# Router scores of two expert layers: gate matrix as the loaded weights, tokens moving through four column quarters, scores turned on VectorE

## The chip, the cores and the metric

One core of a Trainium2 chip runs the whole kernel as one program. The metric is the device time of one execution in microseconds (us), compared by the median of several runs. TensorE (PE in the profile) multiplies; VectorE (DVE) and ScalarE (ACT) do elementwise work and copies out of PSUM, the memory that TensorE writes; GpSimd (POOL) computes small things and issues gathers; SyncE (SP) issues the plain transfers. PEld is TensorE's loading of weights, which has its own records.

## What is computed

The reference is a chain of six residual layers on 1024 tokens of width 512: a small feed-forward layer with a memory lookup, an attention without softmax, the feed-forward layer again, a mixture of experts, a rotary attention with softmax, and the mixture of experts again. The change touches only the router of the two expert layers:

```python
def _L1_ffn_ref(x, gate_w, w1, w2, w3):        # x: layer-normed tokens, gate_w: 8 x 512
    xt = x.reshape(-1, h)
    logits = xt @ gate_w.T                     # 1024 x 8, in float32
    probs = softmax(logits)
    top_vals, top_idx = top_k(probs, 2)
    top_vals = top_vals / sum(top_vals)
    ...                                        # each token goes through its two experts
```

The kernel takes the two largest of the eight logits of each token (the softmax keeps their order) and derives the two weights from their difference.

## The kernel before

Tokens are cut into `NT` = 8 tiles of `P` = 128, and the width of 512 into `C` = 4 chunks of 128. For each layer k, `HS[k]` is a pair: the normed tokens (token on the partition) and their transpose `HS[k][1]` (channel on the partition, token along the row). Every engine runs a program of its own in a fixed order, written out by hand; engines meet only at semaphores.

The work around the router, tile by tile, is:

- VectorE, in `dve_front`: the residual sum of a tile (L800 before the first expert layer, L1802 before the second), its statistics (L481), aggregation (L492 or L484), and two or three tiles later the normalisation (L488), after GpSimd has given the reciprocal deviation (L568, L569). Two iterations after a tile's normalisation comes `dve_top` for it (L594 and L595: the 8 sorted scores and their indices). The last two tiles' `dve_top` come at the very end; before the first expert layer eight small constants (L503 to L510) stand ahead of them.
- TensorE, in `pe_front` (L602): four transposes of a normed tile into PSUM; ScalarE copies them into `HS[k][1]` (L610). Then `pe_logits` (L586): for each of the four chunks one matmul whose weights are the 128 x 128 token block and whose moving operand is 8 columns of `gateT`. The result is 128 tokens by 8 scores, in the layout that `dve_top` reads directly.
- The order on TensorE before the first expert layer, in `pe_ffn0`: logits of tile i-2, then transposes of tile i, for i = 2 to 7, then logits of tiles 6 and 7. Before the second, in `pe_attn1`: four wide matmuls of the attention's output projection (L1675) for tile i-1, logits of tile i-5, transposes of tile i-4.
- `top_bank` gives two PSUM banks in turn; logits of tile i wait until `dve_top` of tile i-2 is done (`s_top`).

A float32 matmul instruction leaves two loads and two matmul records in the trace.

Behind the last `dve_top` comes the routing, one chain: `dve_moe` on VectorE (from L1224 on) ranks all tokens, TensorE inverts the permutation (L1090 to L1101), GpSimd gathers the first rows (L1056), they are transposed (L1107), and the experts begin (L1123). All engines close the layer before with `end_stage` on `stage_end`; SyncE then waits for `s_lgt` and starts to load the last of the four expert streams (L956, L967). [...]

`gateT` is stored 32 columns wide (`SR` = 32): columns 0 to 7 hold the gate matrix, the rest is zero. `NSTR` is 4. `NB32`, a tile of 256 words per partition, is used only later, in `dve_moe`.

Of the kernel before, what the change touches and what calls it, by code (L numbers as in the profile page):

```python
# [14 lines left out]
P = 128  # L15
T, D = 1024, 512
NT = T // P
C = D // P
# [15 lines left out]
NE, FF, TOPK = 8, 800, 2  # L34
SR = 32
NSTR = P // SR
# [13 lines left out]
def macaron_program(nc, A, out, stages=6):  # L50

    ctx = ExitStack()
    with ctx:
        def sb(name, shape, dt=F32):
            return ctx.enter_context(nc.sbuf_tensor(name, shape, dt))
# [48 lines left out]
        gateT = sb("gateT", [P, C, SR])  # L104
# [22 lines left out]
        PS = ctx.enter_context(nc.psum_tensor("PS", [P, 8, PSUM_F], F32))  # L127
# [14 lines left out]
        def S(name):  # L142
            if name not in sems:
                sems[name] = sem(name)
            return sems[name]
# [44 lines left out]
        HS = [(H1, HT1), (H1, HT1), (H2, HT2), (H2, HT2), (H1, HT1), (H1, HT1)]  # L190
# [42 lines left out]
        at = 2 * D + 2 * C * P  # L233
# [7 lines left out]
        def rtake(shape, dt=F32, parts=P):  # L241
            n = int(np.prod(shape))
            words = n if dt in (F32, U32) else (n + 1) // 2
            ap = RT[0:parts, rt[0]:rt[0] + words]
            rt[0] += words
            assert rt[0] <= 1160
            if dt != F32:
                ap = ap.bitcast(dt)
            if len(shape) > 1:
                names = "abcdefg"[:len(shape)]  # L250
                ap = ap.rearrange(f"p ({' '.join(names)}) -> p {' '.join(names)}",
                                  **{k: v for k, v in zip(names, shape)})
            return ap
# [9 lines left out]
        NB32 = rtake([NE, T // SR])  # L263
# [41 lines left out]
        at = 7584 + 2 * (2 * C * FF + FC * D)  # L305
# [159 lines left out]
        def instance(k):  # L465

            return SL[:k].count(SL[k])
# [4 lines left out]
        def dve_front(eng, link, k, update):  # L472


            lag = BEHIND[k]
            for n in range(NT + lag):
                if n < NT:
                    update(n)
                if 0 <= n - 1 < NT:
                    eng.wait_ge(s_x, NT * k + n)  # L480
                    eng.bn_stats(STAT[:, n - 1, :], X[:, n - 1, :]).then_inc(s_stat, 1)  # L481
                if n == NT and k == 5:
                    eng.wait_ge(s_stat, NT * k + n)
                    eng.bn_aggr(MV[:, n - 1, :], STAT[:, n - 1, :]).then_inc(s_moments, 1)  # L484
                if 0 <= n - lag < NT:
                    i = n - lag
                    eng.wait_ge(s_rstd, NT * k + i + 1)
                    eng.tensor_scalar(HS[k][0][:, i, :], X[:, i, :], MV[:, i, 0:1], RS[:, i:i + 1],  # L488
                                      ALU.subtract, ALU.mult).then_inc(s_h, 1)
                if 0 <= n - 1 < NT and not (n == NT and k == 5):  # L490
                    eng.wait_ge(s_stat, NT * k + n)
                    eng.bn_aggr(MV[:, n - 1, :], STAT[:, n - 1, :]).then_inc(s_moments, 1)  # L492
                if SL[k] == "moe" and n >= lag + 2:
                    dve_top(eng, link, k, n - lag - 2)
            if SL[k] == "moe":
                if instance(k) == 0:
                    dve_route_constants(eng, link)
                for i in range(NT - 2, NT):
                    dve_top(eng, link, k, i)
# [71 lines left out]
        def top_bank(k, i):  # L571

            return ((7, 4), (6, 7))[instance(k)][i % 2]

        def pe_logits(eng, k, i):

            f = instance(k)
            if f == 0 and i == 0:
                eng.wait_ge(S("s_gate"), 16)
                eng.wait_ge(S("s_sgl"), SL[:k].count("ffn0"))  # L580
                eng.wait_ge(S("s_ewc"), 2 * SL[:k].count("ffn0"))
            eng.wait_ge(s_ht, NT * k + i + 1)
            if i >= 2:
                eng.wait_ge(S("s_top"), NT * f + i - 1)
            for c in range(C):
                mm = eng.matmul(PS[:, top_bank(k, i), 0:NE], HS[k][1][:, c, i * P:(i + 1) * P], gateT[:, c, 0:NE],  # L586
                                start=(c == 0), stop=(c == C - 1))
            mm.then_inc(S("s_lgt"), 1)

        def dve_top(eng, link, k, i):  # L590
            f = instance(k)
            eng.wait_ge(S("s_lgt"), NT * f + i + 1)
            scores = PS[:, top_bank(k, i), 0:NE]
            link(eng.max(V8[:, i, :], scores))  # L594
            eng.max_index(I8[:, i, :], V8[:, i, :], scores).then_inc(S("s_top"), 1)  # L595

# [30 lines left out]
        def pe_ffn0(eng, k, f):  # L627
# [64 lines left out]
            for i in range(2, NT):  # L692
                if SL[k + 1] == "moe":
                    pe_logits(eng, k + 1, i - 2)
                pe_front(eng, k + 1, i)
            if SL[k + 1] == "moe":
                for i in range(NT - 2, NT):
                    pe_logits(eng, k + 1, i)
# [896 lines left out]
        def pe_attn1(eng, k):  # L1595
# [66 lines left out]
            for i in range(NT + 1):  # L1662
                if i < NT:
                    if i >= 2:
                        eng.wait_ge(S("s_ott"), i - 1)
                    for c in range(C):
                        tr = eng.transpose(PS[:, i % 2, c * P:(c + 1) * P], OTM[:, i, c * P:(c + 1) * P], ident[:])
                    tr.then_inc(S("s_ottr"), 1)
                j = i - 1
                if 0 <= j < NT:  # L1670
                    eng.wait_ge(S("s_ott"), j + 1)
                    if j >= 2:
                        eng.wait_ge(s_x, NT * (k + 1) + j - 1)
                    for c in range(C):
                        mm = eng.matmul(PS[:, 4 + j % 2, :], OTT[:, c, j * P:(j + 1) * P], WO[:, c, :],  # L1675
                                        start=(c == 0), stop=(c == C - 1))
                    mm.then_inc(S("s_wop"), 1)
                if i >= 5:
                    pe_logits(eng, k + 1, i - 5)
                if i >= 4:  # L1680
                    pe_front(eng, k + 1, i - 4)
# [261 lines left out]
```

## Time and profile before

| | us |
|---|---|
| median of 3 runs | 1244.46 |
| lowest and highest | 1243.29, 1249.1 |
| the profiled execution, its own time | 1242.31 |
| its span, from first to last instruction | 1240.5 |
| TensorE busy | 1152.3 (93% of the span) |
| VectorE busy | 866.3 (70%) |
| ScalarE busy | 352.7 (28%) |

Busy shares are means over stages with different limits. To judge an edit in two short stretches (about 160 to 179 us and 870 to 896 us), one reads these stretches: the chain of waits through them, and the instructions in order of time on TensorE and VectorE. [...]

### The profile page before, as it was taken

How to read it: one execution, taken by the hardware profiler on the slowest of the kernel's cores; microseconds unless marked ns; L12 is line 12 of the kernel's file. 1: busy time of each engine (PE TensorE's matmuls, PEld its weight loads, DVE VectorE, ACT ScalarE, POOL GpSimd, SP SyncE). 2: the span in 40 equal slices, each digit the busy share in tenths (PEclk: the TensorE clock that was granted, in tenths of full speed). 3: DMA queues.
4: the chain of work that ended last, by engine and by line, in shares of the span. 5: the costliest groups of instructions: out<-in, count | busy, mean ns of one | idle time of the engine just before them, and what ended most of it. 6: DMA issues, size and time to landing. Idle time of an engine off the chain costs nothing.

```text
span 1240.5 us, 28148 instructions
## 1 busy us (share of the span) xinstructions
PE 1152.3 (93%) x9930; PEld 521.7 (42%) x9930; DVE 866.3 (70%) x2483; ACT 352.7 (28%) x746; POOL 147.9 (12%) x223
## 2 busy tenths in 40 slices
PE   6799987999999999899899999999979899999992
PEld 3478563443333333444344444444624333333330
DVE  5832675877777774578889999942458678777754
ACT  5444610001010101322176777784110010101010
POOL 2220011011010101344000000000110010101010
PEclk9899979999999999999999999999899999999996
DMA  9100433158723436418704333006741655616566
GB/s 359 59 2 1 158 137 130 37 184 287 259 98 96 167 124 211 180 62 180 170 3 87 53 53 53 2 2 251 301 177 36 246 176 189 216 36 215 168 204 251
DMA packets 63668, 174.33 MB, mean 141 GB/s; under 512 B 9885, under 2 KB 16627, under 8 KB 61351
## 3 DMA queue, kind: packets, MB, share of 16 engines
q1 hardware_dynamic: 55471, 150.60, 37.5%
q0 software_dynamic: 5760, 18.88, 4.3%
q10 hardware_dynamic: 2296, 3.05, 0.7%
q8 instruction: 79, 1.29, 0.4%
q14 instruction: 62, 0.51, 0.1%
HBM read 785.47 MB, written 22.03 MB: 651 GB/s over the span
## 4 chain that ended last, share of the span: by engine, by line
PE 80%; DVE 9%; DMA 4%; issue 2%; ACT 2%; SPq 1%; POOL 0%; POOLq 0%; ACTq 0%; DVEq 0%
PE PS L1123 30%; PE PS L1142 14%; PE PS L1648 6%; PE PS L1635 5%; PE PS L1613 5%; PE PS L837 3%; PE PS L822 2%; PE PS L1675 2%; PE PS L1563 2%; PE PS L602 2%; DVE PS L1771 2%; PE PS L1568 1%; PE PS L586 1%; PE PS L1638 1%; DMA HH<-in_w 1%
## 5 line engine op out<-in xcount | busy, mean ns | idle before, releaser
L1123 PE MATMUL PS<-arena 128*32 128x400 f32 x3456 | 397.4, 502 | 8.1 <-DMA HH<-in_w 4.2
L1123 PE MATMUL PS<-HH,arena 128*32 128x400 f32 x1152 | 396.7, 502 | 0.0
L1123 PEld LDWEIGHTS PS<-arena 128*32 128x32 f32 x3456 | 147.3, 111 | 246.9 <-issue 238.8
L1313 DVE STREAM_TRANSPOSE arena<-arena 32x192 f32<-32x192 f32 x576 | 211.4, 367 | 7.2
L1771 DVE CUSTOM_DVE_ANT_0 PS<-PS,U 128x128 f32<-128x128 f32 (+7 forms) x256 | 186.7, 786 | 15.4 <-PE PS L1613 15.0
L1142 PE MATMUL PS<-arena 128*32 128x512 f32 x1512 | 192.3, 592 | 4.0 <-DVE arena L1313 4.0
L1291 DVE STREAM_TRANSPOSE arena<-arena 32x128 f32<-32x128 f32 x544 | 164.7, 303 | 16.7 <-DMA arena<-h_scratch,RT 8.8
L1718 ACT ACTIVATE arena<-PS 128x512 f32<-128x512 f32 (+3 forms) x384 | 160.1, 512 | 54.9 <-PE PS L1638 48.2
L1196 ACT ACTIVATE arena<-PS 128x400 f32<-128x400 f32 x72 | 36.2, 504 | 422.3 <-PE PS L1123 422.2
L1297 DVE TENSOR_TENSOR arena<-arena,PS 128x400 f32<-128x400 f32 x72 | 40.9, 571 | 128.6 <-ACT arena L1196 128.5
L1123 PEld LDWEIGHTS PS<-HH,arena 128*32 128x32 f32 x1152 | 126.1, 111 | 0.0
L1142 PEld LDWEIGHTS PS<-arena 128*32 128x32 f32 x1512 | 57.6, 110 | 123.7 <-issue 117.6
L1635 PE MATMUL PS<-arena 99*128 99x512 bf16 (+3 forms) x384 | 106.8, 328 | 1.1 <-ACT arena L1718 1.0
L1613 PE MATMUL PS<-arena 96*128 96x512 bf16 (+3 forms) x384 | 97.0, 327 | 2.8 <-DVE arena L1771 1.0
L1142 PE MATMUL PS<-HH,arena 128*32 128x512 f32 x216 | 98.6, 592 | 0.0
L1056 POOL DMA_INDIRECT arena<-h_scratch,RT x36 | 34.9, 968 | 376.7 <-DVE arena L1291 327.5
L1648 PE MATMUL PS<-arena 128*32 128x512 f32 (+3 forms) x768 | 76.2, 494 | 0.2 <-ACT HH L1725 0.2
L1635 PEld LDWEIGHTS PS<-arena 99*128 99x128 bf16 x384 | 36.7, 97 | 58.2 <-ACT arena L1718 26.9
L1066 POOL DMA_INDIRECT y_scratch<-arena,RT x36 | 35.3, 980 | 210.1 <-ACT arena L1208 205.9
L568 POOL TENSOR_SCALAR VE<-MV 128x1 f32<-128x1 f32 (+1 forms) x44 | 12.2, 277 | 403.6 <-DVE MV L492 368.4
L1563 PE MATMUL PS<-HH,arena 128*128 128x512 f32 x128 | 57.3, 608 | 1.7 <-ACT HH L610 0.9
L1208 ACT COPY arena<-PS 128x512 f32<-128x512 f32 x36 | 20.3, 587 | 121.9 <-PE PS L1156 73.5
(258 smaller groups left out, 1253.2 us busy)
## 6 DMA issues: line engine op xcount, KB each, us to landing
arena<-in_w SPq DMA_DIRECT2D x456, 800.0 KB
arena<-in_w2a SPq DMA_DIRECT2D x266, 768.0 KB
HH<-in_w SPq DMA_DIRECT2D x152, 800.0 KB
HH<-in_w2a SPq DMA_DIRECT2D x38, 768.0 KB
arena<-split_scratch SPq DMA_DIRECT2D x96, 128.0 KB, 6.3
arena<-y_scratch SPq DMA_DIRECT2D x24, 256.0 KB, 5.3
split_scratch<-arena SPq DMA_DIRECT2D x8, 768.0 KB, 4.8
arena<-in_wqkv SPq DMA_DIRECT2D x3, 1024.0 KB, 6.3
```

The lines of the kernel that those rows point to most:

```text
L837: mm = eng.matmul(PS[:, bank, jj * P:(jj + 1) * P], AT0[:, m % 4, j * P - a:(j + 1) * P - a], h_in[:, i, h * P:(h + 1) * P], start=(i == 0 ...
L1123: mm = eng.matmul(PS[SR * j:SR * j + SR, 2 * hf + m, 0:FH], XBT[:, u, c, SR * j:SR * j + SR], W13[j][:, c // 2, m, c % 2, hf * FH:(hf + 1) ...
L1142: mm = eng.matmul(PS[SR * j:SR * j + SR, y_bank(p), :], ACT_T[:, u, c, SR * j:SR * j + SR], half_of(j, half)[:, c % (FC // 2), :], start=( ...
L1291: tr = eng.transpose(XBT[SR * b:SR * b + SR, u, :, SR * a:SR * a + SR], src[:, :, SR * b:SR * b + SR])
L1297: eng.tensor_tensor(half, half, PS[:, 2 * hf + 1, 0:FH], ALU.mult).then_inc(S("m_act"), 1)
L1313: tr = eng.transpose(ACT_T[SR * b:SR * b + SR, u, :, rows], src[:, :, SR * b:SR * b + SR])
L1563: mm = eng.matmul(PS[:, at + par, :], WQKV[:, x, c, first:first + P], HS[k][1][:, c, J * HT_:(J + 1) * HT_], start=(c == 0), stop=(c == C ...
L1613: mm = eng.matmul(PS[:, b + lo // HT_, 0:hi - lo], QT[0:KS, slot, h, i * P:(i + 1) * P], KT[0:KS, slot, h, lo:hi], start=True, stop=True)
L1635: mm = eng.matmul(bank[:, 0:hi - lo], KT[0:KS + 3, slot, h, i * P:(i + 1) * P], QT[0:KS + 3, slot, h, lo:hi], start=True, stop=not diag, s ...
L1648: mm = eng.matmul(PS[32 * h:32 * h + 32, 7, lo - J * HT_:HT_], VA[:, i, (GH * g + h) * VC:(GH * g + h) * VC + 32], PB[n % NPB][:, h, 0:hi ...
L1718: eng.activation(PB[(n // GH) % NPB][:, h, 0:hi - lo], PS[:, EXP_BANK[u], 0:hi - lo], ACT.Exp, scale=SCALE1).then_inc(S("s_p"), 1)
L1771: eng.tensor_tensor_reduce(scores, scores, MASKW[:, T - wide:T], 1.0, HOLE, ALU.add, ALU.max, MP[:, g % 2, h, i:i + 1]).then_inc(S("s_md"), 1)
```

## The change

In `pe_logits` the operands change places. The weights are now the chunk of the gate matrix, 128 x 32, and the moving operand is 32 tokens of the transposed tile. The tile's 128 tokens are split in four groups; group j uses output partitions 32j to 32j+31, and with them a quarter of the array's columns. So a chunk takes four matmul instructions and a tile sixteen, where it took four. The result in PSUM is turned: partition 32j+e holds the score of expert e, column t the token 32j+t. `dve_top` therefore begins with one more VectorE instruction, which transposes each 32 x 32 block from PSUM into a part of `NB32`; `max` and `max_index` read that.

```diff
@@ pe_logits
             for c in range(C):
-                mm = eng.matmul(PS[:, top_bank(k, i), 0:NE], HS[k][1][:, c, i * P:(i + 1) * P], gateT[:, c, 0:NE],
-                                start=(c == 0), stop=(c == C - 1))
+                for j in range(NSTR):
+                    at = i * P + SR * j
+                    mm = eng.matmul(PS[SR * j:SR * j + SR, top_bank(k, i), 0:SR], gateT[:, c, :], HS[k][1][:, c, at:at + SR],
+                                    start=(c == 0), stop=(c == C - 1), skip_group_check=True)
             mm.then_inc(S("s_lgt"), 1)
@@ dve_top
             eng.wait_ge(S("s_lgt"), NT * f + i + 1)
-            scores = PS[:, top_bank(k, i), 0:NE]
+            turned = NB32.rearrange("p e b -> p (e b)")[:, SR * i:SR * i + SR]
+            link(eng.transpose(turned, PS[:, top_bank(k, i), 0:SR]))
+            scores = turned[:, 0:NE]
             link(eng.max(V8[:, i, :], scores))
             eng.max_index(I8[:, i, :], V8[:, i, :], scores).then_inc(S("s_top"), 1)
```

`link` makes the next VectorE instruction wait until this one is complete. No instruction changes its place among the others. On TensorE before the first expert layer, transposes (first row and third) alternate with the logits of a tile. Before:

```order
L602 MATMUL PS<-ident,arena 128x128 x4
L586 MATMUL PS<-gateT,arena 128x8 x4
L602 MATMUL PS<-ident,arena 128x128 x4
L586 MATMUL PS<-gateT,arena 128x8 x8
L1090 MATMUL PS<-RT,trib 128x72
```

and now:

```order
L606 MATMUL PS<-ident,arena 128x128 x4
L588 MATMUL PS<-arena,gateT 32x32 x16
L606 MATMUL PS<-ident,arena 128x128 x4
L588 MATMUL PS<-arena,gateT 32x32 x32
L1094 MATMUL PS<-RT,trib 128x72
```

The 4 instructions of a tile became 16 at the same place, the 8 of the last two tiles 32. On VectorE, in the same stretch, an iteration of `dve_front` with its `dve_top` was:

```order
L488 TENSOR_SCALAR arena<-X,MV,RS 128x512
L492 BN_AGGR MV<-STAT 128x2
L594 MAX RT<-PS 128x8
L595 MAX_INDEX RT<-RT,PS 128x8
L800 SCALAR_TENSOR_TENSOR X<-PS,arena,X 128x512
```

and is now:

```order
L488 TENSOR_SCALAR arena<-X,MV,RS 128x512
L492 BN_AGGR MV<-STAT 128x2
L596 STREAM_TRANSPOSE RT<-PS 128x32
L598 MAX RT<-RT 128x8
L599 MAX_INDEX RT<-RT 128x8
L804 SCALAR_TENSOR_TENSOR X<-PS,arena,X 128x512
```

The transpose stands between the tile's aggregation and its `max`, 16 times in the program. ScalarE, GpSimd and SyncE keep their programs.

## Rows read from the trace of the kernel before

**Rows 1.** Chain that ended last, 150 to 215 us: start us, us, what.

```profile
162.71 0.65 DVE X L800
...
167.69 1.51 PE PS L586 x8
...
178.31 0.19 DVE RT L594
...
178.96 0.30 DVE RT L1224
```

**Rows 2.** The same chain, 840 to 930 us.

```profile
870.71 0.79 PE PS L586 x8
...
892.43 3.23 PE PS L586 x16
...
896.34 0.30 DVE RT L1224
```

**Rows 3.** Stretches: us, busy of PE, PEld, DVE, ACT, POOL; then granted clock.

```profile
155.00:166.00 11.00, 8.30 (x49) 5.51 (x47) 10.29 (x30) 2.35 (x4) 4.49 (x11) 1.00 0.25 95
166.00:179.00 13.00, 11.69 (x56) 11.59 (x56) 6.06 (x35) 2.35 (x4) 1.58 (x4) 0.50 0.22 81
197.00:200.00 3.00, 3.00 (x20) 0.85 (x16) 2.88 (x10) 0.61 (x1) 0.40 (x1) 0.50 0.29 87
```

**Rows 4.** VectorE and ScalarE in order of time: start us, us, what [idle before <-releaser].

```profile
162.26 0.17 DVE L594 MAX8 RT<-PS 128x8 f32<-128x8 f32 x1 [0.54 <-PE PS L586]
...
162.62 0.73 DVE L800 SCALAR_TENSOR_TENSOR X<-PS,arena,X 128x512 f32<-128x512 f32 x1
...
889.94 0.55 DVE L488 TENSOR_SCALAR HH<-X,MV,RS 128x512 f32<-128x512 f32 x1 [0.40 <-POOL RS L569]
...
175.09 0.59 ACT L610 COPY arena<-PS 128x512 f32<-128x512 f32 x1 [1.87 <-PE PS L602]
```

**Rows 5.** TensorE in order of time, 166 to 179 us, same columns.

```profile
169.05 1.09 PE L602 MATMUL PS<-ident,arena 128*128 128x128 f32 x4
169.94 1.72 PE L586 MATMUL PS<-gateT,arena 128*128 128x8 f32 x8
...
173.96 1.09 PE L602 MATMUL PS<-ident,arena 128*128 128x128 f32 x4
```

**Rows 6.** TensorE, 200 to 201 us: three of four quarters in two rounds.

```profile
200.43 0.51 PE L1123 MATMUL PS<-arena 128*32 128x400 f32 x3
...
200.77 0.51 PE L1123 MATMUL PS<-arena 128*32 128x400 f32 x3
```

**Rows 7.** TensorE, 273.9 to 274.7 us: first and last of 16 in a burst.

```profile
274.01 0.61 PE L1156 MATMUL PS<-arena,ACT_RING 32*32 32x512 f32 x1
...
274.12 0.61 PE L1156 MATMUL PS<-wu1T,ACT_RING 32*32 32x512 f32 x1
```

**Rows 8.** TensorE, 844 to 846.1 us: quarters (L1648) and whole array in turn.

```profile
843.67 1.04 PE L1648 MATMUL PS<-arena 128*32 128x512 f32 x8
844.64 0.28 PE L1635 MATMUL PS<-arena 99*128 99x256 bf16 x1
...
845.73 0.23 PE L1635 MATMUL PS<-arena 99*128 99x128 bf16 x1
845.80 0.22 PE L1638 MATMUL PS<-mask_st,identb 128*128 128x128 bf16 x1
845.95 1.50 PE L1648 MATMUL PS<-arena 128*32 128x384 f32 x24
```

**Rows 9.** VectorE by form: busy us, mean ns | idle before: its transposes.

```profile
L1291 DVE STREAM_TRANSPOSE arena<-arena 32x128 f32<-32x128 f32 x544 | 164.7, 303 | 16.7 <-DMA arena<-h_scratch,RT 8.8
L1310 DVE STREAM_TRANSPOSE ACT_RING<-arena 32x32 f32<-32x32 f32 x144 | 29.2, 203 | 2.7
```

**Rows 10.** TensorE, 187.4 to 188 us: small matmuls on the whole array.

```profile
187.44 0.57 PE L1101 MATMUL PS<-arena 128*128 128x54 bf16 x16 [2.73 <-DVE arena L1257]
187.86 0.38 PE L1085 MATMUL PS<-identb 128*128 128x512 bf16 x1
```

## The prediction

> **What bounds the kernel now.** TensorE is the busiest engine over the whole span, but an edit in two short stretches is judged there, so the first view is the chain of waits through the stretches in which the routers work.
>
> Before the first expert layer [rows 1] the chain runs on VectorE up to about 166.6 us (its rows are sums, statistics and normalisations like the first one shown). From there to 178.31 it is on TensorE without a break: transposes and router matmuls in turn, 1.51 us for a tile of logits. Before the second layer [rows 2] it is on TensorE earlier, where projections alternate with tiles of logits of 0.79 us; the last two tiles of logits take 3.23. Both times the routing (L1224, at 178.96 and 896.34) starts only when the last tile is ranked, and nothing of the experts can start before it.
>
> [...] In the slow stretch weight loading is busy 11.59 of 13 us: these matmuls cost the loading of 128 columns of tokens; their 8 moving columns are nothing beside it. The change goes at the right term.
>
> The third view is TensorE in order of time [rows 5]: a period is (173.96 - 169.05)/2 = 2.46 us, of which the transposes have 0.89 and a tile of logits 1.56, counted from start to start. By the same way of counting 0.79 at full clock is some 0.82.
>
> **What a tile of logits costs afterwards.** Sixteen instructions make 32 pairs, in 8 rounds of four quarters. The trace has no pair with 32 loaded and 32 moving columns, so I bound it. The experts' quarters take 0.34 us a round for 400 columns [rows 6], by columns 0.027 for 32. A load of 32 columns is a quarter of the 0.10 us (0.79/8) of one of 128, 0.025. Starts are 7 ns apart: 16 small pairs start from 274.01 to 274.12 [rows 7], 0.027 for four. All three agree if load, matmul and starts overlap; I take 0.03 a round and 0.24 for eight. The upper end are 16 whole-array matmuls of 54 and 36 columns, which take 0.42 us, 26 ns each whatever their columns [rows 10]: 32 x 0.026 = 0.83.
>
> Changing between whole array and quarters has a price too. L1638, with 128 bf16 columns (half of the 0.12 that 256 need), is followed by the first quarter of L1648 after 0.15: 0.09 more than its columns. The other way, L1635 starts 0.97 after the first of two rounds of 512 columns, each 0.34 x 512/400 = 0.43: 0.11 more [rows 8]. I take 0.19 a tile. A block is 0.19 + 0.24 = 0.43 against 0.82: **0.39 saved at full clock**. At half clock I double the rounds (0.45, without margin) and take 0.30 for the two changes, between 0.19 and 0.38: 0.75 against 1.55, **0.80 saved**.
>
> **What the transpose costs.** VectorE turns 32 x 32 elements in 203 ns and 32 x 128 in 303 [rows 9]. Here it is 32 elements per partition, on all partitions and out of PSUM; with `link` around it I take 0.24 us, the ends being 0.20 and 0.37. Maximum and index take 0.36 us (162.26 to 162.62, [rows 4]) as before, so a ranking is 0.60.
>
> **First expert layer.** In the VectorE part three transposes add 0.72. Against it, VectorE waits 0.54 us for the first logits [rows 4], and that block ends 0.39 earlier: net +0.33 by 167 us. Only +0.1 of it reaches tile 4's transposes on TensorE, since the third transpose lies behind that tile's normalisation. The next tile's normalisation comes late by another 0.1. Then three periods of 0.90 + 1.55 become 0.90 + 0.75: -2.4. The loop through VectorE (logits, ranking, normalisation, next transposes) comes close behind TensorE within the same period. From the last transposes (173.96) to the last ranking (178.31) were 4.35 us. Now ScalarE's copy is waited for: it ends at 175.68 [rows 4], 1.72 after those transposes start; the last logits follow with 0.7, and latencies make it 2.5. VectorE's constants and the ranking before the last end at the same time. That is -1.85, and the last transpose adds 0.24. Sum: 0.2 - 2.4 - 1.85 + 0.24 = **-3.8 us**.
>
> **Second expert layer.** TensorE is the bound for the logits of tiles 0 to 2, between projections: 3 x 0.39 = -1.15. Then VectorE's iterations lead, with one more transpose in them, and tile 7's normalisation, at 889.94 before [rows 4], comes about 0.87 earlier. From it to L1224 were 6.4 us, most of it TensorE at half clock. Now it is 0.6 for the normalisation, 1.78 for transposes and copy, 0.7 for the logits, and 0.65 (178.31 to 178.96 in [rows 1]) + 0.24 for the ranking: 3.97, or -2.43. Sum **-3.3 us**.
>
> **What follows.** The routing, the gather and SyncE's load of the last weight stream all start on the end of the last ranking, so they shift together. Total -7.1: the profiled execution would take 1242.31 - 7.1 = 1235.2. It is 2.15 below the median of the three runs, so the median becomes 1244.46 - 7.1 = **1237.3**.
>
> **Rivals.**
>
> A. *The pair has a floor.* If each pair costs the 26 ns of [rows 10] in quarters too, and twice that at half clock, a block is 0.83 + 0.19 = 1.02 against 0.82, and 1.66 + 0.30 = 1.96 against 1.55. Some 5 blocks count at full and 8 at half clock, and 1.7 us of transposes: 5 x 0.2 + 8 x 0.41 + 1.7 = +6.0, **1250.5, slower than before**. If the floor does not double, 8 x (1.13 - 1.55) = -3.4 and the total is -0.7, 1243.8. The same sum, 1.7 - 5 x 0.63 - 8 x 1.25 + (5 + 16) x 32p, turns from gain to loss at p = 0.017 us a pair. Against it: 7 ns in [rows 7], though that is a burst of 16, not 32. Chance 0.12.
>
> [...]
>
> B. *Load and matmul of one quarter do not overlap* when both are this short: a round takes twice as long, 13.5 ns a pair. The same sum gives -2.4, 1242.1. For it: no row shows the overlap with so few columns. Chance 0.14.
>
> C. *The clock.* TensorE does less here, so the clock may fall one stretch earlier (0.5 and 0.9 us), or the experts' first matmuls, at half clock from 197 to 200 [rows 3], may stay there for longer, 1.7 us each time. That leaves 2.5 to 5.5 of the gain: 1239 to 1242. Chance 0.16. Experts that start at full clock would give 1.5 to 3 more instead, down to 1234; that is in my range.
>
> D. *It moves nothing*, since the experts' first matmuls wait for something with a time of its own, the weights or the token rows in memory: 1244.5. Against it: the load of the last stream waits for the same event. Chance 0.06.
>
> **Numbers.** The forecast has 0.52. 0.5% is 6.2 us, about what a measurement of this kernel can tell from no change; the border is 1238.2, only 0.9 from the forecast. Most of the forecast's chance and a little of C's lie beyond it: faster 0.50. The rest of the forecast, B, C, D and half of A are within: 0.44. Slower 0.06. The range goes from 1233.5, experts at full clock, to 1244, which leaves out most of A and D.
>
> **What would show it.** L588 as 32 starts a tile about 7 ns apart, blocks of 0.43 us at clock 1.00 and 0.75 at 0.50; a VectorE transpose of 0.20 to 0.25 us; from the start of the first tile's ranking to L1224 13.3 us instead of 16.7; TensorE idle between L588 and L606 in waits for VectorE. Starts 26 ns apart would prove A, 13 ns B, a clock of 0.50 ahead of 166 us or far into the experts C.

## The result, and the profile after

| | before | after |
|---|---|---|
| median of 21 runs of each, us | 1245.96 | 1237.17 |
| lowest and highest, us | 1239.39, 1249.39 | 1231.4, 1247.8 |
| profiled execution, us (span) | 1242.31 (1240.5) | 1238.7 (1236.9) |
| TensorE's granted clock over the span, as a share of its full speed | 0.971 | 0.976 |

The ratio after to before is 0.9938, with a 95% interval of 0.9924 to 0.9952: 7.7 us faster, or 6.0 to 9.5 (the medians differ by 8.8). The forecast was 7.1. Both the size and the sign held; what lies under them held only in part, and the experiments are mostly about that. That the median of 1237.17 lies so close to the 1237.3 forecast is luck in part: the kernel before came out at 1245.96 here, 1.5 above the 1244.46 that the forecast started from. The profiled execution was forecast at 1235.2 and took 1238.7.

First the chain that ended last, after, 150 to 215 us (start us, us, what). It answers to [rows 1].

```profile
165.30 0.44 PE PS L588 x32
165.77 0.23 DVE RT L596
...
172.28 0.66 PE PS L606 x4
172.94 0.44 PE PS L588 x32
173.40 0.23 DVE RT L596
...
177.87 0.30 DVE RT L1228
```

TensorE no longer holds the chain without a break. L588 is the new router matmul, L596 the new transpose, L606 the transposes on TensorE (L602 before), L1228 the routing (L1224 before). From the first ranking (165.77) to the routing it is 12.1 us; before it was 16.7.

The two stretches can be cut at events that both kernels have: the first from the start of tile 0's transposes on TensorE to the routing, the second from the second layer's first projection to the routing. Here they are for the kernel before (us; busy PE, PEld, DVE, ACT, POOL; then granted clock, DMA share, GB/s):

```profile
157.70:178.96 21.26, 18.24 (x100) 16.66 (x100) 13.65 (x56) 4.69 (x8) 4.73 (x12) 0.70 0.26 99
851.08:896.34 45.26, 43.79 (x184) 27.87 (x184) 17.68 (x57) 8.35 (x15) 6.51 (x16) 0.93 0.89 356
```

The same view of the kernel after:

```profile
161.57:177.87 16.30, 10.08 (x292) 6.67 (x292) 15.06 (x65) 4.69 (x8) 4.83 (x12) 1.00 0.36 132
849.65:891.19 41.54, 38.30 (x376) 20.33 (x376) 19.23 (x64) 8.36 (x15) 6.51 (x16) 1.00 0.97 388
```

The first stretch is 4.96 us shorter, the second 3.72. Weight loading has gone from 16.66 to 6.67 us and from 27.87 to 20.33; VectorE does 1.4 to 1.55 us more. What the sum of the forecast did not have is the last column but two, the granted clock: 0.70 and 0.93 before, 1.00 and 1.00 in this execution after. [rows 3] showed 13 us at half clock around the end of the first stretch; here there is none ahead of either routing.

The stretches shrink by 8.7 us together, the profiled executions differ by 3.6 only. The rest lies where nothing was changed: the first stretch begins at 157.70 before and at 161.57 after, and over the fourteen profiled executions told of here its start lies anywhere from 157.70 to 164.54. All that lies outside the two stretches adds up to 1171.2 to 1180.4 us over the fourteen (1174.0 before, 1179.1 after). So the stretches are the finer ruler below, with two limits: each kernel has one profile, and the time from a routing to the experts, which is told of further down, is not in them.

TensorE in order of time, after (start us, us, engine line, matmul, out<-in, count [idle before <-releaser]):

```profile
165.23 0.46 PE L588 MATMUL PS<-arena,gateT 128*32 128x32 f32 x32
165.62 0.66 PE L606 MATMUL PS<-ident,arena 128*128 128x128 f32 x4
166.21 0.46 PE L588 MATMUL PS<-arena,gateT 128*32 128x32 f32 x32
168.21 0.66 PE L606 MATMUL PS<-ident,arena 128*128 128x128 f32 x4 [1.55 <-DVE arena L488]
```

A block of 32 pairs is 0.39 us from its start to the next transposes' start (165.23 to 165.62). Record by record, the four quarters of a round start 7 ns apart and the next round starts 32 ns after the last one did (52 ns after the first round of a block). The last line has the wait that the prediction asked for: TensorE idle until VectorE's normalisation. Summed up by who is waited for, 161 to 178 us (waiting <- released by: us, times, longest):

```profile
PE PS L606 <- DVE arena L488: 5.2, 6, 1.5
```

and before, 157 to 179 us:

```profile
DVE RT L594 <- PE PS L586: 6.9, 6, 1.6
```

The wait has turned round. Before, VectorE stood 6.9 us waiting for logits and TensorE 3.3 us waiting for normalised tiles; now VectorE waits 0.2 us and TensorE 5.2.

VectorE in order of time, after, answering to [rows 4], and its transposes grouped by form (busy us, mean ns | idle before):

```profile
165.77 0.22 DVE L596 STREAM_TRANSPOSE RT<-PS 128x32 f32<-128x32 f32 x1 [0.17 <-PE PS L588]
166.02 0.17 DVE L598 MAX8 RT<-RT 128x8 f32<-128x8 f32 x1
...
166.38 0.73 DVE L804 SCALAR_TENSOR_TENSOR X<-PS,arena,X 128x512 f32<-128x512 f32 x1
```

```profile
L596 DVE STREAM_TRANSPOSE RT<-PS 128x32 f32<-128x32 f32 x16 | 3.2, 200 | 0.9 <-PE PS L588 0.8
```

A ranking takes 0.61 us (165.77 to 166.38); 0.60 was forecast.

### The profile page after: what moved, and what is told of

Same layout as the page of the kernel before. It is cut to its first block, busy times and chain, and to the rows that moved or that the text cites. A ratio compares the mean times of both kernels' runs of the same rounds, so it can differ in the third digit from the quotient of the medians.

```text
span 1236.9 us, 28932 instructions
## 1 busy us (share of the span) xinstructions
PE 1143.9 (92%) x10314; PEld 505.7 (41%) x10314; DVE 869.3 (70%) x2499; ACT 352.8 (29%) x746; POOL 147.9 (12%) x223
## 4 chain that ended last, share of the span: by engine, by line
PE 77%; DVE 11%; DMA 5%; issue 2%; ACT 2%; SPq 2%; POOL 1%; POOLq 0%; ACTq 0%; DVEq 0%
PE PS L1127 30%; PE PS L1146 14%; PE PS L1652 6%; PE PS L1639 5%; PE PS L1617 5%; PE PS L841 3%; PE PS L826 2%; PE PS L1679 2%; DVE PS L1775 2%; PE PS L1572 1%; PE PS L606 1%; PE PS L1642 1%; DMA HH<-in_w 1%; DMA arena<-y_scratch 1%; PE PS L1160 1%
## 5 line engine op out<-in xcount | busy, mean ns | idle before, releaser
L1146 PE MATMUL PS<-arena 128*32 128x512 f32 x1512 | 195.7, 600 | 4.0 <-DVE arena L1317 4.0
L1295 DVE STREAM_TRANSPOSE arena<-arena 32x128 f32<-32x128 f32 x544 | 164.7, 303 | 15.7 <-DMA arena<-h_scratch,RT 7.8
L1146 PE MATMUL PS<-HH,arena 128*32 128x512 f32 x216 | 101.8, 608 | 0.0
```

Source lines behind the costliest of these rows:

```text
L1146: mm = eng.matmul(PS[SR * j:SR * j + SR, y_bank(p), :], ACT_T[:, u, c, SR * j:SR * j + SR], half_of(j, half)[:, c % (FC // 2), :], start=( ...
L1295: tr = eng.transpose(XBT[SR * b:SR * b + SR, u, :, SR * a:SR * a + SR], src[:, :, SR * b:SR * b + SR])
```

## The experiments

All fourteen kernels by the same two stretches. "Half" is the time at clock 0.50 worked out of the granted clock, 2 x (1 - clock) x length. Each row is one profiled execution; the ratio is of all executions to those of the kernel before, with its 95% interval.

| kernel | first stretch, us (clock, half) | second, us (clock, half) | ratio |
|---|---|---|---|
| before | 21.26 (0.70, 12.8) | 45.26 (0.93, 6.3) | 1 |
| the change | 16.30 (1.00, 0) | 41.54 (1.00, 0) | 0.9938 [0.9924, 0.9952] |
| e1, first layer only | 17.46 (0.80, 7.0) | 45.62 (0.92, 7.3) | 0.9934 [0.9910, 0.9958] |
| e2, second layer only | 21.59 (0.65, 15.1) | 41.54 (1.00, 0) | 0.9952 [0.9933, 0.9971] |
| e3, before and a transpose ahead of each ranking | 22.01 (0.69, 13.6) | 45.56 (0.93, 6.4) | 1.0002 [0.9984, 1.0020] |
| e4, a quarter after the other | 17.40 (1.00, 0) | 43.37 (1.00, 0) | 0.9914 [0.9882, 0.9946] |
| e5, before with 32 columns | 21.33 (0.69, 13.2) | 42.56 (0.99, 0.9) | 0.9989 [0.9970, 1.0008] |
| e6, before with 128 columns | 16.29 (1.00, 0) | 42.80 (1.00, 0) | 0.9924 [0.9901, 0.9946] |
| e7, constants early | 17.20 (0.80, 6.9) | 41.55 (1.00, 0) | 0.9959 [0.9941, 0.9977] |
| e8, the change again | 17.46 (0.80, 7.0) | 42.19 (0.95, 4.2) | 0.9957 [0.9938, 0.9975] |
| e9, padded | 15.79 (1.00, 0) | 41.54 (1.00, 0) | 0.9936 [0.9914, 0.9957] |
| e10, 128 columns, constants early | 16.29 (1.00, 0) | 42.80 (1.00, 0) | 0.9933 [0.9907, 0.9958] |
| e11, 128 columns, then the change | 16.29 (1.00, 0) | 41.54 (1.00, 0) | 0.9924 [0.9903, 0.9946] |
| e12, e6 again | 16.29 (1.00, 0) | 42.80 (1.00, 0) | 0.9947 [0.9923, 0.9970] |

### One layer at a time: e1 and e2

```diff
-            for c in range(C):
-                for j in range(NSTR):
...
+            if f == 0:
+                for c in range(C):
+                    for j in range(NSTR):
...
+            else:
+                for c in range(C):
+                    mm = eng.matmul(PS[:, top_bank(k, i), 0:NE], HS[k][1][:, c, i * P:(i + 1) * P], gateT[:, c, 0:NE],
```

and in the same way in `dve_top`; e2 has `f == 1`.

> The turned scores in the first expert layer only; the second keeps the old form. In the two profiles so far the stretch from the first transposes to the routing in the first layer took 21.3 us before (12.9 of them at half clock) and 16.3 after (none at half clock). Theory (each router chain is shortened by itself, because TensorE at half clock or the projection was its bound): this kernel gains the first layer's share of the forecast, 3.8 us, ratio about 0.997; its first stretch takes 16.3 to 17.5 us, its second (from the first projection matmul to the routing) stays at 45.3 when half of the tail is at half clock, less when not. Rival (the gain is the clock's: one execution before had the bad stretch, one after had the good one): the ratio is within 0.001 of 1 and the first stretch swings between 16 and 21 whichever form it has.

> The turned scores in the second expert layer only. Theory: gain 3.3 to 3.7 us, ratio about 0.997; the stretch from the first projection matmul to the routing takes 41.5 to 42.5 us against 45.3; the first layer's stretch behaves as before, about 21 us when at half clock. The two parts add up to the whole change (0.9938). Rival (gain of the clock): ratio near 1 and no stable difference in this stretch.

Each layer keeps its own part. Where the old form stands, the stretch is as before within 0.4 us (45.62 against 45.26; 21.59 against 21.26) and so, roughly, is its clock; where the new one stands, 17.46 and 41.54. The parts by the stretches are 3.80 and 3.72 us. Both ratios look larger than 3.8 us in 1245 (0.9970), e1's even with its whole interval, and the two together would make 14 us (8.8 at least, by their intervals) where the change has 7.7 (9.5 at most). Part of the excess lies behind the routings, where both profiles were quick (see below): with these parts e1 gains 5.8 us and e2 4.0 over the profile before, and their intervals begin at 5.2 and 3.6. The change itself came out at 0.9938 and, in e8, at 0.9957, so differences of 2 us between such ratios say little.

### The transposes alone: e3

```diff
             scores = PS[:, top_bank(k, i), 0:NE]
+            turned = NB32.rearrange("p e b -> p (e b)")[:, SR * i:SR * i + SR]
+            link(eng.transpose(turned, X[:, i, 0:SR]))
             link(eng.max(V8[:, i, :], scores))
```

Each ranking turns 32 x 32 blocks of X beside what it did; nobody reads the result. That makes eight a layer, sixteen in all.

> The kernel before with one more VectorE transpose of 128 x 32 ahead of each ranking, of data that nobody reads, so only the cost of the added instruction. The ranking still waits for the logits first, so the transpose stands on the path as in the change. Theory: 0.21 to 0.24 us each; on the path are three in VectorE's part of the first layer (partly hidden behind TensorE), and one at the end of each layer, so +0.5 to +1.7 us, ratio 1.0004 to 1.0014. Rival (VectorE is not the bound anywhere there, so the transposes are free): only the last one of each layer, below +0.5.

VectorE's transposes of this kernel, by form:

```profile
L595 DVE STREAM_TRANSPOSE RT<-X 128x32 f32<-128x32 f32 x16 | 3.2, 199 | 9.3 <-PE PS L586 9.3
```

199 ns each from SBUF, 200 from PSUM: no price for reading PSUM here. The first stretch is 0.75 us longer than before and the second 0.30. But the old form without them has 21.26 to 21.59 (before, e2) and 45.26 to 45.62 (before, e1), so what the transposes cost is 0.4 to 0.75 us in the first and nothing that shows in the second, not 16 x 0.24 = 3.8: VectorE had waits for logits to hide them in. The ratio cannot resolve 1 us.

### The order of the pairs: e4

```diff
-            for c in range(C):
-                for j in range(NSTR):
+            for j in range(NSTR):
+                for c in range(C):
```

> The change with its two loops exchanged: all four chunks of a quarter, then the next quarter. The same 32 pairs a tile, but successive pairs are in the same quarter. Theory (the block is short because four quarters load and multiply side by side, 32 ns a round of four in the profile after): neighbouring pairs of one quarter must follow each other by about 30 ns, the block grows from 0.25 to 0.9 or 1.0 us at full clock, and the whole gain of TensorE goes: +0.7 us a tile, +5 to +8 us against the change, ratio to before 0.999 to 1.002. Rival (TensorE reorders or overlaps pairs freely whatever their order): the block stays near 0.25 us and the ratio at 0.994.

The same 32 pairs, but all of a quarter's ahead of the next quarter's. TensorE in order of time:

```profile
163.39 0.90 PE L588 MATMUL PS<-arena,gateT 128*32 128x32 f32 x32
164.22 0.66 PE L606 MATMUL PS<-ident,arena 128*128 128x128 f32 x4
```

The block takes 0.83 us from start to start instead of 0.39. Record by record, pairs of one quarter follow each other every 32 ns, which is exactly a round's time in the change: a quarter takes 32 ns for a pair in both, and the order decides how many work at once. Here neighbouring quarters overlap only at their ends: each starts 0.15 us after the one before, when that one has three of its eight pairs still to start. So the gain of a block is the overlap of the quarters. I had expected that this would cost the whole gain and it did not: the stretches are longer than the change's by 1.10 and 1.83 us only, and the ratio, 0.9914 from six executions, is even the lowest of all, with an interval that takes in the change's. By the stretches it should be 3 us behind the change; whole runs do not resolve that. The block is as long as the old one at full clock (0.82), and yet 5.75 of the 8.68 us stay, beside a clock of 1.00. That was the first sign that the block's length at full clock was not what paid.

### What the moving columns do to the clock: e5, e6 and e12

[rows 3] has TensorE busy for 11.69 of 13 us, nearly all of it covered by weight loading, at half clock. These leave the old form, its loads and its order alone and move more columns of the router's matrix than are read, e5 32 instead of 8:

```diff
-                mm = eng.matmul(PS[:, top_bank(k, i), 0:NE], HS[k][1][:, c, i * P:(i + 1) * P], gateT[:, c, 0:NE],
+                mm = eng.matmul(PS[:, top_bank(k, i), 0:SR], HS[k][1][:, c, i * P:(i + 1) * P], gateT[:, c, 0:SR],
```

and e6, with e12 its repetition, 128, by moving the same 32 four times:

```diff
+                mm = eng.matmul(PS[:, top_bank(k, i), 0:P].rearrange("p (a b) -> p a b", a=NSTR),
+                                HS[k][1][:, c, i * P:(i + 1) * P], gateT[:, c:c + 1, :].broadcast_to([P, NSTR, SR]),
```

> The kernel before, whose router matmuls move all 32 columns of gateT (24 of them zero) instead of 8. Each pair is bound by the load of 128 columns, 0.10 to 0.11 us at full clock, so the wider movement costs TensorE nothing (0.82 us a tile as before). So far the granted clock fell to half in every profile inside a router chain of the old form (166.0, 171.0, 168.8 us in the first layer; 889.7, 887.5, 895.8 in the second) and in the turned form once out of six. Theory M (the clock falls in the old form because its matmuls move next to nothing): with 32 columns it falls later or not at all; the first stretch goes from 21.3 towards 17.5 us, ratio 0.995 to 0.999. Rival L (the clock has nothing to do with the columns moved; turned scores win by shorter blocks): nothing changes, ratio 1.000, half clock as before.

> The same with 128 columns moving (gateT four times, by a step of zero), which still hides behind the load: 128 columns take 0.107 us at full clock. Theory M: the clock stays at 1.00 in both router chains; the first stretch takes 17 us or less, the second about 43.5, ratio 0.993 to 0.995, as good as the change although nothing is turned and TensorE's work per tile is as long as before. Rival L: as the kernel before, ratio 1.000, or slower where the loads and the wider movement collide.

> The kernel before with 128 columns moving, once more, with a profile of its own. Theory M (the old form loses its time to the half clock, and the clock falls because next to nothing moves): ratio 0.992 to 0.995, no half clock in either chain, stretches 16.3 and 42.8 us. Rival (the first result was a lucky execution): ratio 0.998 to 1.0, half clock again in one of the chains.

The stretches of e6:

```profile
162.01:178.30 16.29, 13.42 (x100) 11.44 (x100) 13.65 (x56) 4.69 (x8) 4.79 (x12) 1.00 0.34 129
848.53:891.33 42.80, 41.48 (x184) 25.37 (x184) 17.74 (x56) 8.34 (x15) 6.51 (x16) 1.00 0.94 377
```

and TensorE at the end of the first one, where [rows 5] has the kernel before at half clock:

```profile
173.85 0.60 PE L603 MATMUL PS<-ident,arena 128*128 128x128 f32 x4
174.28 1.06 PE L586 MATMUL PS<-gateT,arena 128*128 128x128 f32 x8
175.18 0.60 PE L603 MATMUL PS<-ident,arena 128*128 128x128 f32 x4
175.61 2.00 PE L586 MATMUL PS<-gateT,arena 128*128 128x128 f32 x16
```

A tile of logits is 0.90 us (174.28 to 175.18) where it was 0.82 at full clock and 1.56 at half. Sixteen times the columns cost 0.08 us, and the clock stays at 1.00 in all four kernels whose chain is in this form (e6, e10, e12 and e11's first layer): 16.29 us each time. Without turning anything, e6 has 0.9924 and e12 0.9947, the same as the change within their intervals.

With 32 columns the first stretch is as before, at 0.69, and the second nearly at full clock: 0.99 and 42.56 us. Its ratio shows no gain of note. I had not expected the two stretches to differ.

One profile a kernel is little, but the granted clock over the whole span is on record for every execution. Its mean is 0.9657, 0.9680 and 0.9669 for the kernel before (24, 25 and 15 executions), 0.9685 with 32 columns (12), and 0.9775, 0.9773 and 0.9751 with 128 columns (6, 6 and 8: e6, e10, e12). So the higher clock of the wide form is no accident of the profiled executions.

### The constants, and padding: e7, e8, e9

e7 moves VectorE's eight instructions of routing constants, which stand ahead of the last two rankings, to where VectorE waits anyway, long before:

```diff
-                if instance(k) == 0:
-                    dve_route_constants(eng, link)
...
             if f == 0:
                 dve_binds(eng, link)
+            else:
+                dve_route_constants(eng, link)
```

e9 does so too and fills TensorE's waits with matmuls whose output nobody reads, here before the first expert layer:

```diff
                     pe_logits(eng, k + 1, i - 2)
+                    if i >= 3:
+                        pe_awake(eng, 0, (3, 3, 1, 0, 0)[i - 3])
```

and one or two before each of the last three `pe_front` ahead of the second. e8 is the change, unaltered.

> The change, and VectorE's eight constants for the routing (L503 to L510, 1.2 us) are computed in the feed-forward layer before, where VectorE waits, instead of ahead of the last two rankings of the first expert layer. Theory (VectorE is the bound of the first router chain after the change): the last but one ranking starts as soon as its logits are there, the stretch goes from 16.3 to 15.6 us, ratio to the kernel before 0.0005 below the change's. Rival (the last copy of ScalarE and the last logits are the bound): nothing.

> The change itself once more, on the same chip and in the same rounds as the three others, and with a profile of its own. Expected: ratio 0.9938 as measured, within its interval of 0.9924 to 0.9952; first stretch 16.3 to 17.5 us, second 41.5; no half clock inside the router chains or one short stretch.

> The change with early constants, and matmuls that feed nothing where TensorE waits for VectorE: 3, 3 and 1 ahead of the transposes of tiles 3, 4 and 5 in the first layer, 2, 2 and 1 ahead of those of tiles 5, 6 and 7 in the second, 0.21 us each at full clock, into a PSUM bank that is free there. Theory (a part of the executions of the change lose 1 to 2 us to a stretch at half clock inside the chain, as two of four profiles of the turned form show in the first layer; the fillers keep the clock up): full clock in both chains, first stretch 15.7 us, second 41.5 to 42, ratio 0.992 to 0.994. Rival (the fillers delay the transposes by as much as the clock gives): ratio as the change on this chip, 0.994 to 0.996.

The stretches of e8:

```profile
160.55:178.01 17.46, 12.41 (x292) 8.44 (x292) 15.09 (x64) 4.68 (x8) 4.83 (x12) 0.80 0.33 122
848.56:890.75 42.19, 39.30 (x376) 21.09 (x376) 19.32 (x64) 8.35 (x15) 6.51 (x16) 0.95 0.95 383
```

The same program as the change, and its first stretch has 7 us at half clock, as e1's and e7's. Of the four profiles whose first layer is the change's without padding (the change, e1, e7, e8), only the change's own kept the clock at 1.00. The clocks over the span have both outcomes too: of the 21 executions of the change eleven had 0.970 to 0.972, like e8's profile (0.971), and ten 0.975 to 0.978, like the profiled one (0.976). TensorE in order of time inside it:

```profile
171.25 1.12 PE L606 MATMUL PS<-ident,arena 128*128 128x128 f32 x4 [0.34 <-DVE arena L488]
172.30 0.66 PE L588 MATMUL PS<-arena,gateT 128*32 128x32 f32 x32
172.89 1.12 PE L606 MATMUL PS<-ident,arena 128*128 128x128 f32 x4
```

A period is 1.64 us (171.25 to 172.89); 2.46 was the old one, and 1.65 had been forecast. So the change has both outcomes, a clock that holds and one that falls for a while; it costs 1.16 us in the first stretch (17.46 against 16.30) and 0.65 in the second (42.19 against 41.54). The constants are worth 0.26 us in a stretch of the same clock (17.20 against 17.46), where 0.7 was expected, and nothing in the ratio. The padded kernel has 1.00 in both and the shortest first stretch, 15.79 (15.7 had been expected), and a mean clock over the span of 0.9761 (8 executions; 0.9740 for the change, 0.9713 in e8), but its ratio is the change's.

### Combinations: e10 and e11

e10 is e6 with e7's constants. e11 has the old form with 128 columns in the first layer, the turned form in the second, and the constants early; both edits are shown above.

> The kernel before with 128 columns moving, and the constants early. In its profile without early constants TensorE was back to back in the tail of the first layer at full clock. Theory: TensorE is the bound there, so early constants change nothing, first stretch 16.3 us, second 42.8, ratio 0.992 to 0.994. Rival (VectorE is the bound): 0.5 us better.

> The form with 128 columns moving in the first layer, where it held the clock, and the turned form in the second, where TensorE is the bound at full clock and the shorter block counts; constants early. Theory: first stretch 16.3 us with no half clock, second 41.5, ratio 0.991 to 0.993, the best of all by about 1 us. Rival: no better than either form alone, since the clock in the chains already was full in most executions.

e10's first stretch is e6's to the hundredth, so in the old form, where TensorE sets the end, the constants cost nothing. e11 has the better of both, 16.29 and 41.54, the lowest median of all (1235.94 us) and a ratio whose interval overlaps the change's; the 1 us that had been expected over the others is not shown. No kernel here is shown to be faster than the change.

## Why the prediction was right, point by point

**The term that the change goes at.** Right: weight loading of 128 columns filled the slow stretch, 166 to 179 us at a granted clock of 0.50 [rows 3], and over the first stretch of the ruler it has gone from 16.66 to 6.67 us. The same eight pairs of load and matmul took 0.79 us where the clock was 1.00 [rows 2] and 1.51 where it was 0.50 [rows 1]. One reading of [rows 1] was a little wide: up to 166.6 us the chain before is not on VectorE throughout, it has transposes, feed-forward matmuls and one tile of logits from 159.91 to 162.24.

**The block.** The mechanism held and the size was a little off. TensorE in order of time, second layer, after: from a projection into a block, and out of it into transposes.

```profile
867.83 1.45 PE L1679 MATMUL PS<-arena,HH 128*128 128x512 f32 x3
869.21 0.46 PE L588 MATMUL PS<-HH,gateT 128*32 128x32 f32 x32
869.60 0.66 PE L606 MATMUL PS<-ident,HH 128*128 128x128 f32 x4
870.09 0.60 PE L1671 MATMUL PS<-ident,HH 128*128 128x128 f32 x4
```

From the start of this block to the next one's (874.05) are 4.84 us; in the kernel before the same way is 5.16 (870.54 to 875.70), both at clock 1.00. A block saves 0.32 at full clock, not 0.39, so it costs 0.50 and not 0.43. Its eight rounds are 0.26 of that, as forecast (0.24); the two changes between whole array and quarters make the other 0.24 where 0.19 was taken. Entering is seen in the first two lines: 1.38 us for three projection matmuls, and 1.29 in e6, which stays on the whole array (866.71 to 868.00). At half clock the forecast was exact: a period of 1.64 against 1.65, so 0.82 saved against 0.80.

**The transpose.** 0.20 us busy, 0.22 to 0.25 with what `link` adds, forecast 0.24.

**First layer, -3.8.** The sum goes by a clock that falls in this stretch as in [rows 3]. Where it does, in e1 and e8, the stretch is 17.46 us, from 21.26: -3.80. It holds term by term in e8, counted from the start of the stretch: the transposes of tile 4 start 0.12 us later than before (0.2 was forecast), the three periods from there to tile 7's take 4.97 us instead of 7.38 (-2.41; forecast -2.4), and from there to the routing it is 3.49 instead of 5.00 (-1.51; forecast -1.61). (The clock falls about 170 us in e8 instead of 166, while TensorE still waits for VectorE.) The time from the first ranking to the routing is 13.27 us in e8 (164.74 to 178.01), and 13.3 was forecast. In the profiled execution of the change the clock stayed up, and it was 12.1: -4.96 for the stretch. There VectorE ended up as the bound: TensorE waits 5.2 us for normalised tiles, VectorE 0.2 for logits. The kernel that moves 128 columns takes the same 16.29 us with TensorE back to back at its end; that the two agree to the hundredth is chance, for with the constants early they take 15.79 (e9, padded) and 16.29 (e10).

**Second layer, -3.3.** Measured -3.72 with the clock at 1.00 (after, e2, e7) and -3.07 with 4 us of it at half (e8). Three blocks between projections gave 3 x 0.32 = 0.96 where 1.15 was forecast. With that, tile 7's normalisation came 0.68 us earlier in the stretch, 0.87 was forecast. From it to the routing it was 6.4 us, 3.97 were forecast from rows at half clock, and in e8, at half clock too, it is 4.01 (886.74 to 890.75). With the clock up it is 3.36, in the last lines of VectorE's trace after:

```profile
887.83 0.55 DVE L488 TENSOR_SCALAR HH<-X,MV,RS 128x512 f32<-128x512 f32 x1 [0.16 <-POOL RS L569]
...
889.55 0.22 DVE L596 STREAM_TRANSPOSE RT<-PS 128x32 f32<-128x32 f32 x1 [0.57 <-PE PS L588]
...
891.19 0.29 DVE L1228 TENSOR_TENSOR RT<-small,RT 128x128 f32<-128x128 f32 x1 [0.20 <-DVEq L160]
```

**What follows shifts along.** Right in the main, so rival D falls, but not to the hundredth. From the first routing to the experts' first matmul it is 17.41 us before and 16.13 after, in e8 16.31; from the second 17.71, 17.82 and 17.86. The 1.1 to 1.3 us of the first are not the clock's: the chain up to there is as long in both (10.60 us) until the gather of token rows, which takes 5.43 us before and 4.16 after. The difference repeats. All six kernels with turned scores in the first layer have 16.13 to 16.31, all eight with the old form 17.34 to 17.69. What goes with it in the trace is one DMA packet of 16 KB that brings instructions. The DMA view of the kernel before, 178.96 to 196.3 us, has it (packets, MB, share of 16 engines):

```profile
q8 instruction: 1, 0.02, 0.3%
```

and the same view of the kernel after, 177.87 to 194 us, has no such row. The packet takes 0.93 us and falls 10 us after the routing, into the last weight stream, whose end is 1.2 us later with it (14.92 against 13.72 us after the routing). Over both layers of all fourteen profiles, the time from routing to experts is 17.34 to 18.17 us in the 20 cases with such a packet between the routing and the stream's end, and 16.13 to 16.86 in the 8 without one. It isn't the form of the scores: the old form in e1's second layer escapes the packet, with 16.55, and the turned form in the second layer of the change doesn't. So the change gains some 1.2 us here, most likely because its added TensorE instructions move that packet out of the way; this is argued from where the packets fall, not shown by a run of its own. The forecast had no such term.

**Rival A, a floor of 26 ns a pair,** is refuted: starts are 7 ns apart within a round, and the 32 pairs take 0.26 us from the first start to the last, 8.5 ns each.

The 26 ns of [rows 10] were measured on the whole array. Pairs on different quarters start closer than that, 7 ns apart; pairs on one quarter, 32 ns apart in e4, start further apart.

**Rival B, no overlap of a quarter's load and matmul,** expected 13.5 ns a pair or 54 a round; a round takes 32. Refuted.

**Rival C, the clock,** was where the argument was weakest. I had it as a loss, a clock that falls earlier than before. It went the other way: the old form with 8 columns is what loses the clock, in each of its six stretches (0.70 and 0.93 before, 0.92 in e1's second, 0.65 in e2's first, 0.69 and 0.93 in e3). In all four first stretches of the old form with 8 or 32 moving columns the clock was at 0.65 to 0.70 (before, e2, e3, e5), in all four with 128 columns at 1.00 (e6, e10, e11, e12), with the same number of loads (100 in the stretch) and the same tiles. That the half clock stays in both chains is a premise that both sums use ("8 at half clock" in rival A) and nothing argues for beyond [rows 3]; it is the step that did not hold in the profiled execution, and that did hold in part in e8.

How much of the gain is the clock? With the clock at 1.00 in both, the change is worth nothing over the wide old form in the first stretch (16.29 against 16.30) and 1.26 us in the second (42.80 against 41.54). The whole is 4.96 + 3.72 = 8.68 us, of which e6 has 4.97 + 2.46 = 7.43. So a kernel that only keeps the clock has 7.4 of the 8.7 us, but lacks the 1.2 us behind the first routing (17.48 in e6). Where the clock falls, as in e8, the shorter block pays instead, with 3.80 + 3.07 = 6.87 us. The two causes stand in for one another, and that is why a forecast that knew only one of them came so close. That it came within 0.6 us is luck in part: it left out both what the clock gives back in about half of the executions and the 1.2 us of the packet.

What stays open: why the same program keeps the clock in the first stretch in one profiled execution (the change) and loses it in another (e8), why 32 moving columns keep it in the second stretch and not in the first, and whether the packet of instructions is the cause of the 1.2 us. That the moving columns decide is shown by e6 and e12 against before (1.00 against 0.70 in the first stretch, 1.00 against 0.93 in the second); by what measure they do is not.

## What to carry to other kernels

Where TensorE is at half clock in a stretch full of weight loads, try more moving columns in the same matmuls before any rewriting; here 128 instead of 8 cost 0.08 us a tile and brought 7.4 us by the stretches, and ratios of 0.9924 to 0.9947 by whole runs, while 32 left the first stretch at a clock of 0.69 (e5). Making the small operand the weights, a quarter of the columns each, took the block here from 0.82 us to 0.39, start to start, with the quarters taking turns within each round, and to 0.83 with one quarter after the other (e4). Before a gain behind the edit is put down to it, look where the packets of instructions fall in both traces. And when whole runs scatter by some 5 us either way, as they did here, compare stretches between events that both programs have.

## What the runs showed of the hardware

- Pairs of load and matmul with 32 loaded and 32 moving fp32 columns, at clock 1.00: 32 ns apart on one quarter (e4, 163.4 to 164.2 us), 7 ns between quarters and 32 ns a round (after, 165.2 to 165.5 us). At clock 0.50 a round took 53 ns (e8, 172.3 us).
- From the whole array into quarters and back, 0.24 us together at clock 1.00: an estimate, what is left of a block of 0.50 us beside its eight rounds of 0.26 (second layer, 867.8 to 874.1 us after against 870.5 to 875.7 before).
- The same 100 weight loads in the first stretch, 64 of them the router's and 32 for transposes, went with different clocks: 0.70 with 8 columns moving in the router's 64 matmuls (before), 0.69 with 32 (e5), 1.00 with 128 (e6, e10, e12). The loads were busy for 16.66 us before and 11.44 in e6.
- A VectorE transpose of 128 x 32 fp32 took 200 ns from PSUM (after) and 199 from SBUF (e3).
- A packet of 16 KB of instructions within the weight stream went with more time from the routing to the experts, 17.41 us against 16.13 behind the first routing (before, after): 17.34 to 18.17 us in 20 cases with it, 16.13 to 16.86 in 8 without. No run shows that it is the cause.
